# Feed-forward norm without its mean, scale and shift on the activations: one transposed set for two products

## The chip, the cores and the metric

One core of one Trainium2 chip runs the whole program. The metric is the device time of one execution in microseconds (us). Engines: TensorE (PE, matmuls and transposes), VectorE (DVE), ScalarE (ACT), GpSimd (POOL), and the queue that issues the DMAs (SP). All data are fp32.

## The reference

Eight images of 32x32 positions with 128 channels go through two layers. Layer 0: layer norm, full self-attention over the 1024 positions with 8 heads of 16, output product, residual. Layer 1, on the same 1024 tokens:

```
tokens = x @ Win + b_in
t      = layernorm(tokens) * g1 + be1          # queries, pooled keys and values
attn   = attention of all queries on the 16 best of 64 pooled keys
tokens = tokens + attn                         # "tok2" in the kernel
t2     = layernorm(tokens) * g2 + be2
ff     = gelu(t2 @ Wf1 + bf1) @ Wf2 + bf2
out    = (tokens + ff) @ Wout + bout
```

with layernorm(x) = (x - mean) * rsqrt(var + 0.001). The kernel computes out as tok2 @ Wout + gelu(...) @ (Wf2 @ Wout) + a constant row (`out_bias`), with Wf2 @ Wout (`w2o`) folded at the start.

## The kernel before, in words

An image's 1024 tokens are 8 tiles of 128, its heads 4 pairs. The main loop `image(n)` of each engine runs over n = 0 to 7 and, inside, over 32 steps s (a pair of heads times a tile of keys). At each step TensorE makes the attention scores of image n (L636, into the tile S, in two halves c), ScalarE takes their exponentials (L904, Pr), and TensorE multiplies these with V (L651, O; in most images for two steps together, in images 0, 7 and the start of 1 for one). Into every step other work is woven, in an order written out by hand and the same on all engines:

- `before_tasks(n, s)`: layer 0's norm, transposes and products of image n + 1 (input transposes L584 at steps 6 and 10, evicted by ScalarE to xhT and xnT; the product `tokx`, by `by_token` L665 with A<-win_s, drained by VectorE at L1049 at steps 32 and 37, that is steps 0 and 5 of the next loop). The transposes of step 6 reuse PSUM bank A and wait for that drain.
- `after_tasks(n, s)`: layer 1 of image n. Its steps 0 to 31 run in the loop of image n + 1, its steps 32 to 43 in the loop of image n + 2. The step numbers are in the tuples USUAL (images 0 to 5) and ENDING (images 6 and 7). After the last loop, `tail()` lists the steps that are left: image 6's 32 and 33, image 7's 0 to 3, image 6's 34 to the end, then image 7's. Image 7 (LAST) works by itself there, its TensorE kept busy by matmuls without use (L888, WARM).

Each engine executes its own instructions in this order; semaphores tie the engines together. Layer 1's products go through two PSUM banks, BC[0] and BC[1], in turns numbered by `b_turns`: `b_turn` makes TensorE wait until the turn before on that bank is drained, `drain_b` makes an evicting engine wait until it is filled.

The end of layer 1, for image n < 7, in USUAL's step numbers:

- `tok` (3): the product of the attention output with `wow` (L665, BC<-wow,attnT) gives the tokens. It waits for the DMAs (SP, L366) that bring the attention output of the image whose loop has just ended, in transposed form, after `divide_o` (L1130 to L1137) on VectorE. VectorE adds (L1158), takes statistics (L1019) and makes mean and 1/deviation in some eighteen operations on 128x8 values (`layer_norm`, L1026 to L1043), into ln1; `norm1` (8) normalises (L1146, eight operations).
- `tok2` (31): VectorE adds the layer-1 attention to the tokens, in a tile that shares E2's memory (the profile prints E); statistics. `layer_norm` again at 32, into the same ln1.
- `tt2` (33): eight transposes of the raw tokens tok2 (L657, BC<-ident,E), copied by ScalarE into tok2T, a name for Y's memory (L932, Y<-BC). ScalarE first waits for the store of the image before (out_done).
- `norm2` (34): VectorE writes `that` = (tok2 - mean) / deviation (L1146). `t2` (37): eight transposes of it (L657, BC<-ident,that), and ScalarE's evictions into tT multiply by g2 and add be2 (L919).
- `ff` (39): TensorE's products with Wf1 (L765), VectorE's evictions with bf1 into hT (L1302), ScalarE's gelu (L953) with a table load before and behind.
- `wout` (40): tok2T times Wout into both BC banks (L772). `out` (41 and 43): hT times w2o is accumulated on top (L780), one bank each, and VectorE evicts with `out_bias` into Y (L1311). SP stores Y in the next loop.

In ENDING the same steps are tt2 29, norm2 30, t2 32, ff 33, wout 34, out 35 and 36; image 7 accumulates its output in A and O.

## Time and profile before

| | us |
|---|---|
| median of 3 runs (lowest, highest) | 808.82 (807.91, 809.05) |
| the profiled execution | 811.36 |
| its span, first to last instruction | 809.6 |
| mean granted TensorE clock in it | 0.985 |
| busy: TensorE, ScalarE, VectorE, GpSimd | 762.6, 605.2, 503.5, 162.2 |
| exponentials L904, 512 of them, mean | 1029 ns |
| loop of image 3, by the starts of its exponentials | 282.5 to 374.6 |

The rows in the section further down are copied from the profile. A row of the timeline gives the start and the length of a merged group of instructions in us, then the engine, the line, the operation, what it writes and reads with the shapes, how many there are, and in brackets the idle time of the engine before it and what ended it. "issue" stands for idle time that no other engine's work ended. TensorE's fp32 products show as two instructions each. Times run from the first instruction.

### The profile page before, as it was taken

To read this page: it belongs to the slowest core of one execution; us is meant where nothing else is said; L and a number is where in the kernel's file an instruction comes from. 1 tells how busy PE (TensorE), PEld (TensorE's weight loads), DVE (VectorE), ACT (ScalarE), POOL (GpSimd) and SP (SyncE) were. 2 spreads that over 40 slices of the span, in tenths; PEclk is the share of its full clock that TensorE was granted. 3 is DMA by queue.
4 is the path that set the end of the run, shared out by engine and by line. 5 is a ranking of instruction groups with operands and counts; after the bars stand their busy time and mean duration, and the time that the engine had idled before them with its cause. 6 is when DMAs were issued, how large, how long until landed. Compare 5 with 4: busy or idle time off the path is not lost.

```text
span 809.6 us, 14186 instructions
## 1 busy us (share of the span) xinstructions
PE 762.6 (94%) x5001; PEld 364.6 (45%) x5001; DVE 503.5 (62%) x1512; ACT 605.2 (75%) x686; POOL 162.2 (20%) x198
## 2 busy tenths in 40 slices
PE   7889988999999999999999999999999998999967
PEld 5522333345443545345543555345453544334655
DVE  5512545678657775678657775677736783466764
ACT  3597779787887788787987788878887867876313
POOL 2530503410331221410321212410310201100000
PEclk8999999999999999999999999999999999999979
DMA  2543243532433342522523333422414332400100
GB/s 64 105 81 82 51 67 72 105 51 43 94 69 75 55 69 51 121 51 44 101 54 82 64 57 63 111 49 48 77 36 103 66 53 41 109 9 2 32 1 27
DMA packets 44732, 51.32 MB, mean 63 GB/s; under 512 B 15728, under 2 KB 33776, under 8 KB 44656
## 3 DMA queue, kind: packets, MB, share of 16 engines
q1 hardware_dynamic: 44656, 50.35, 32.2%
q8 instruction: 42, 0.69, 0.4%
q14 instruction: 34, 0.28, 0.1%
HBM read 5.45 MB, written 4.19 MB: 12 GB/s over the span
## 4 chain that ended last, share of the span: by engine, by line
PE 61%; ACT 15%; issue 6%; DVE 5%; ACTq 0%; DVEq 0%
PE O L651 21%; PE S L636 15%; ACT Pr L904 10%; PE BC L665 6%; PE BC L657 3%; PE BC L706 2%; PE BC L765 2%; PE BC L684 2%; PE A L665 2%; PE BC L780 2%; PE A L589 2%; ACT hT L953 1%; ACT L904 1%; ACT L953 1%; ACT E L938 1%
## 5 line engine op out<-in xcount | busy, mean ns | idle before, releaser
L904 ACT ACTIVATE Pr<-S 128x1024 f32<-128x1024 f32 x512 | 491.5, 1029 | 116.0 <-PE S L636 112.3
L651 PE MATMUL O<-Pr,Va 128*32 128x512 f32 x2048 | 255.0, 602 | 1.6 <-DVE OT L1130 0.9
L636 PE MATMUL S<-Qs,Ks 49*128 49x512 f32 x1024 | 216.0, 468 | 23.9 <-ACT Pr L904 21.8
L636 PEld LDWEIGHTS S<-Qs,Ks 49*128 49x128 f32 x1024 | 87.1, 184 | 170.8 <-ACT Pr L904 135.5
L651 PEld LDWEIGHTS O<-Pr,Va 128*32 128x32 f32 x2048 | 49.6, 109 | 103.5 <-issue 95.8
L1130 DVE STREAM_TRANSPOSE OT<-O 128x512 f32<-128x512 f32 x32 | 22.8, 714 | 55.4 <-PE O L651 55.2
L1235 DVE TENSOR_REDUCE r<-BC 128x1 f32<-128x512 f32 x56 | 35.9, 683 | 17.3 <-PE BC L706 17.3
L478 POOL TENSOR_SCALAR xn<-X,ln 128x128 f32<-128x128 f32 x56 | 45.8, 829 | 3.3 <-DVE ln L1043 3.3
L517 POOL TENSOR_TENSOR q1l<-q1T,q1h 128x1024 fp32r<-128x1024 f32 x7 | 16.7, 2381 | 142.1 <-DVE q1h L1187 142.1
L509 POOL TENSOR_TENSOR squares<-qh 128x1024 bf16<-128x1024 f32 x7 | 13.3, 1893 | 153.0 <-DVE hot L1257 112.8
L531 POOL TENSOR_TENSOR tokx<-tokx_new,tok_bias 128x1024 f32<-128x1024 f32 x8 | 18.9, 2366 | 120.0 <-DVE tokx_new L1049 120.0
L919 ACT ACTIVATE tT<-BC,cols 128x512 f32<-128x512 f32 x32 | 23.4, 778 | 22.6 <-PE BC L657 22.6
L500 POOL TENSOR_SCALAR tokx_new<-win_sum,ln 128x128 f32<-128x128 f32 x64 | 37.4, 605 | 1.4 <-POOL tokx L531 1.3
L1302 DVE TENSOR_SCALAR hT<-BC,cols 128x512 f32<-128x512 f32 x28 | 21.0, 751 | 23.2 <-PE BC L765 21.7
L489 POOL COPY Va<-v_new 128x256 f32<-128x256 f32 x32 | 11.8, 399 | 115.0 <-PE O L651 95.2
L1311 DVE TENSOR_TENSOR Y<-BC,out_bias 128x512 f32<-128x512 f32 x14 | 9.6, 690 | 36.5 <-PE BC L780 36.5
L589 PE MATMUL A<-xnT,wqkv_s 128*128 128x512 f32 x56 | 31.5, 645 | 0.0
L765 PE MATMUL BC<-tT,wf_s 128*128 128x512 f32 x56 | 27.5, 614 | 1.1 <-ACT tT L919 0.5
L780 PE MATMUL BC<-w2o,hT 128*128 128x128 f32 x224 | 28.4, 280 | 0.0
L780 PEld LDWEIGHTS BC<-w2o,hT 128*128 128x128 f32 x224 | 26.0, 192 | 4.7 <-issue 4.7
L706 PE MATMUL BC<-Q1s,K1s 96*128 96x512 f32 x56 | 24.1, 510 | 0.0
L1137 DVE STREAM_TRANSPOSE On<-OT 128x512 f32<-128x512 f32 x32 | 22.8, 711 | 1.1
(232 smaller groups left out, 986.9 us busy)
## 6 DMA issues: line engine op xcount, KB each, us to landing
Qs<-qh SPq DMA_DIRECT2D x128, 64.0 KB, 2.3
Ks<-kh SPq DMA_DIRECT2D x128, 64.0 KB, 2.3
Q1s<-q1h SPq DMA_DIRECT2D x56, 128.0 KB, 2.4
X<-in_x_dram SPq DMA_DIRECT2D x8, 512.0 KB, 4.1
Qs<-ql SPq DMA_DIRECT2D x64, 64.0 KB, 2.3
Ks<-kl SPq DMA_DIRECT2D x64, 64.0 KB, 2.3
attnT<-On SPq DMA_DIRECT2D x128, 32.0 KB, 2.0
out_dram<-Y SPq DMA_DIRECT2D x16, 256.0 KB, 2.8
```

The costliest lines, as they stand in the source:

```text
L478: ins = pool.tensor_scalar(xn[:, t, :], X[:, t, :], ln[:, 0, t:t + 1], ln[:, 1, t:t + 1], ALU.subtract, ALU.mult)
L500: ins = pool.tensor_scalar(tokx_new[:, t, :], win_sum[:, :], ln0[n % 2][:, 0, t:t + 1], None, ALU.mult)
L589: pe.matmul(A[:, :], wqkv_s[:, c:c + C], half(xnT, h), start=True, stop=True).then_inc(a_filled, 1)
L636: mm = pe.matmul(S[:, c, a * HALF:(a + 1) * HALF], Ks[head, j, kb * P:(kb + 1) * P], Qs[head, j, c * HALF:(c + 1) * HALF], start=True, sto ...
L651: mm = pe.matmul(O[r:r + 32, :], Va[:, kb, 2 * j + a, :], Pr[:, (STEPS * n + s) % 3, c, a * HALF:(a + 1) * HALF], start=(kb == 0), stop=(k ...
L657: mm = pe.transpose(bank[:, t * P:(t + 1) * P], src[:, 4 * h + t, :], ident[:, :])
L665: mm = pe.matmul(bank[:, t * P:(t + 1) * P], lhs[:, c:c + P], w, start=(i == 0), stop=(i == len(pairs) - 1))
L706: pe.matmul(bank[:, :], K1s[0:ROWS1, j, :, :].rearrange("p a b -> p (a b)"), half(Q1s[0:ROWS1, j, :], h), start=True, stop=True).then_inc( ...
L765: pe.matmul(bank[:, :], wf1_s[:, f * C:(f + 1) * C], half(tT, h), start=True, stop=True)\
L780: mm = pe.matmul(bank[:, t * P:(t + 1) * P], hT[:, f, c:c + P], w2o[:, f, :], start=False, stop=(t == 3 and f == 1))
L904: act.activation(Pr[:, g % 3, c, :], S[:, c, :], ACT.Exp, scale=SCALE).then_inc(probs_ready, 1)
L1235: ins = dve.tensor_reduce(r8[:, 2 * j + h:2 * j + h + 1], bank[:, :], AX.X, ALU.max)
```

## The change

- `scaled_form` takes the place of `normal_form` at norm2: `that` = tok2 / deviation, the mean stays in.
- Since sum over channels of (x - mean) * g2 * Wf1 is a product of x with a weight whose column means are taken off, Wf1 becomes g2 * Wf1 less its column means, and be2 @ Wf1 is added to bf1. That is done once, in the loop of image 1: VectorE scales before the loop, TensorE multiplies by all ones and by be2 at step AT_FOLD = 1, VectorE subtracts and adds.
- The eviction at t2 becomes a plain copy. tT now holds the transposed tokens over their deviation.
- For n < 7 the raw tokens' transposes and copies (tt2) go. `wout` multiplies tT with Wout, in a turn of its own (K_WOUT); VectorE drains it in eight operations that multiply by the deviation (a further result of `layer_norm`, ln2's row 6) and add out_bias, into Y. VectorE, no longer ScalarE, waits for out_done.
- `out` starts its own accumulation, each half in its own turn (K_OUT), and VectorE adds it to Y.
- The second norm's values are in a tile ln2 of their own. Image 7 keeps its raw transposes and its accumulated output, with the changed norm and weight.

```diff
--- before.py
+++ after.py
@@ -96,7 +96,8 @@
 WAKE = 24
 
 K_TOK, K_T, K_Q1, K_PK, K_PV, K_SC, K_RT, K_RB, K_SELK, K_SELV = 0, 2, 4, 6, 7, 8, 16, 17, 18, 19
-K_S2, K_PT, K_TOK2, K_TT2, K_T2, K_FF, K_OUT = 20, 22, 24, 26, 28, 30, 34
+K_S2, K_PT, K_TOK2, K_TT2, K_T2, K_FF, K_OUT, K_WOUT = 20, 22, 24, 26, 28, 30, 34, 36
+AT_FOLD = 1
 FIRST_STEPS = 18
 
 
@@ -122,8 +123,9 @@
                 (at.tt2, K_TT2, 2), (at.t2, K_T2, 2))
     return ((at.tok, K_TOK, 2), (at.t, K_T, 2), (at.q1, K_Q1, 2), (at.pk, K_PK, 2),
             *((at.sc[j], K_SC + 2 * j, 2) for j in range(PAIRS)), (at.rt, K_RT, 1), (at.rb, K_RB, 1), (at.sel, K_SELK, 2),
-            (at.s2, K_S2, 2), (at.pt, K_PT, 2), (at.tok2, K_TOK2, 2), (at.tt2, K_TT2, 2), (at.t2, K_T2, 2),
-            *((at.ff[f], K_FF + 2 * f, 2) for f in range(2)), (at.wout, K_OUT, 2))
+            (at.s2, K_S2, 2), (at.pt, K_PT, 2), (at.tok2, K_TOK2, 2), (at.t2, K_T2, 2),
+            *((at.ff[f], K_FF + 2 * f, 2) for f in range(2)), (at.wout, K_WOUT, 2),
+            (at.out[0], K_OUT, 1), (at.out[1], K_OUT + 1, 1))
 
 
 def b_turns():
@@ -197,7 +199,7 @@
 
         tok, tT, q1T = sb("tok", [P, TILES, C]), sb("tT", [P, T]), sb("q1T", [P, T])
         hT, that = sb("hT", [P, 2, T]), sb("that", [P, TILES, C])
-        st1, ln1 = sb("st1", [P, TILES, 6]), sb("ln1", [P, 8, TILES])
+        st1, ln1, ln2 = sb("st1", [P, TILES, 6]), sb("ln1", [P, 8, TILES]), sb("ln2", [P, 8, TILES])
         pooled, pkv = sb("pooled", [P, POS]), sb("pkv", [POS, 2 * C])
         q1h, q1l = sb("q1h", [P, T], f32r), sb("q1l", [P, T], f32r)
         Q1s = sb("Q1s", [ROWS1 + 1, PAIRS, T], f32r)
@@ -214,6 +216,7 @@
 
 
         E2T = hT[:, 1, :]
+        wf1_scaled = hT[:, 0, 0:FF]
         k1_last = [K1s[:, i, :, :].rearrange("p a k -> p (a k)") for i in range(2)]
         Qt = q1h[:, 0:HALF].rearrange("p (j q) -> p j q", j=PAIRS)
         tok2T, tok2 = Y[:, :, :].rearrange("p t c -> p (t c)"), E2[:, :, :].rearrange("p (t g) k -> p t (g k)", t=TILES)
@@ -258,6 +261,7 @@
         q1h_ready, q1l_ready, q1_stacked = sem("q1h_ready"), sem("q1l_ready"), sem("q1_stacked")
         pooled_ready, hot_ready = sem("pooled_ready"), sem("hot_ready")
         out_done = sem("out_done")
+        ff_scaled, ff_summed, ff_folded = sem("ff_scaled"), sem("ff_summed"), sem("ff_folded")
         last_filled, last_ff, last_out = sem("last_filled"), sem("last_ff"), sem("last_out")
 
         sp_passed, pool_passed, pe_passed, dve_passed = sem("sp_passed"), sem("pool_passed"), sem("pe_passed"), sem("dve_passed")
@@ -668,7 +672,15 @@
 
             def after_tasks(n, s):
                 at = plan(n)
+                if n == 0 and s == AT_FOLD:
+                    pe.wait_ge(ff_scaled, 1)
+                    pe.matmul(BC[0][:, 0:FF], all_ones[:, :], wf1_scaled, start=True, stop=True)
+                    for f in range(2):
+                        mm = pe.matmul(BC[1][:, f:f + 1], wf1_s[:, f * C:(f + 1) * C], BE2, start=True, stop=True)
+                    mm.then_inc(ff_summed, 1)
                 if s == at.tok:
+                    if n == 0:
+                        pe.wait_ge(ff_folded, 1)
                     for side in range(2):
                         pe.wait_ge(attn_in[side], 16 * ATTN_DMAS * (PAIRS // 2) * (n + 1))
                     for h in range(2):
@@ -735,7 +747,7 @@
                     for h in range(2):
                         b_ready(n, K_PT + h)
                         by_token(*b_turn(n, K_TOK2 + h), [(E2T, bd_v[:, :, :].rearrange("p a b -> p (a b)"))], h)
-                if s == at.tt2:
+                if s == at.tt2 and n == LAST:
                     for h in range(2):
                         b_ready(n, K_TOK2 + h)
                         turn4(*b_turn(n, K_TT2 + h), tok2, h)
@@ -766,19 +778,16 @@
                             .then_inc(filled, 1)
                 if s == at.wout and n < LAST:
                     for h in range(2):
-                        bank, filled = b_turn(n, K_OUT + h)
-                        for t in range(4):
-                            c = (4 * h + t) * P
-                            pe.matmul(bank[:, t * P:(t + 1) * P], tok2T[:, c:c + P], wout_s[:, :], start=(t == 0), stop=False)
+                        by_token(*b_turn(n, K_WOUT + h), [(tT, wout_s[:, :])], h)
                 if s in at.out:
                     h = at.out.index(s)
-                    bank, filled = (OUT_BANKS[h], last_filled) if n == LAST else (BC[h], b_filled[h])
+                    bank, filled = (OUT_BANKS[h], last_filled) if n == LAST else b_turn(n, K_OUT + h)
                     for f in range(2):
                         pe.wait_ge(gelu_ready, 2 * n + 1 + f + (2 * h if n == LAST else 0))
                         for t in range(4):
                             c = (4 * h + t) * P
                             mm = pe.matmul(bank[:, t * P:(t + 1) * P], hT[:, f, c:c + P], w2o[:, f, :],
-                                           start=False, stop=(t == 3 and f == 1))
+                                           start=(n < LAST and t == 0 and f == 0), stop=(t == 3 and f == 1))
                     mm.then_inc(filled, 1)
 
             def last_scores():
@@ -913,17 +922,20 @@
             def after_tasks(n, s):
                 at = plan(n)
                 if s in (at.t, at.t2):
-                    g, be, k0 = (G1, BE1, K_T) if s == at.t else (G2, BE2, K_T2)
+                    k0 = K_T if s == at.t else K_T2
                     for h in range(2):
                         bank, drained = drain_b(n, k0 + h)
-                        act.activation(half(tT, h), bank[:, :], ACT.Identity, bias=be, scale=g).then_inc(drained, 1)
+                        if s == at.t2:
+                            act.activation(half(tT, h), bank[:, :], ACT.Copy).then_inc(drained, 1)
+                        else:
+                            act.activation(half(tT, h), bank[:, :], ACT.Identity, bias=BE1, scale=G1).then_inc(drained, 1)
                 if s == at.q1:
                     if n > 0:
                         act.wait_ge(q1_stacked, 16 * STACK1_DMAS * n)
                     for h in range(2):
                         bank, drained = drain_b(n, K_Q1 + h)
                         act.activation(half(q1T, h), bank[:, :], ACT.Copy).then_inc(drained, 1)
-                if s in (at.pt, at.tt2):
+                if s == at.pt or (s == at.tt2 and n == LAST):
                     dst, k0 = {at.pt: (E2T, K_PT), at.tt2: (tok2T, K_TT2)}[s]
                     if s == at.tt2 and n > 0:
                         act.wait_ge(out_done, 2 * 16 * n)
@@ -1136,6 +1148,16 @@
                     dve.wait_ge(attn_in[j % 2], 16 * ATTN_DMAS * (PAIRS // 2 * n + j // 2))
                 dve.transpose(On[:, j % 2, :], OT[:, :, :].rearrange("p q e -> p (q e)")).then_inc(on_ready, 1)
 
+            def scaled_form(own, src, n, k):
+
+                for h in range(2):
+                    dve.wait_ge(b_filled[h], b_after(n, k + h))
+                dve.wait_ge(own[0], own[1] + own[2])
+                for t in range(TILES):
+                    ins = dve.tensor_scalar(that[:, t, :], src[:, t, :], ln2[:, 1, t:t + 1], None, ALU.mult)
+                    if t % 4 == 3:
+                        ins.then_inc(that_ready, 1)
+
             def normal_form(own, src, n, k):
 
                 if n >= 0:
@@ -1151,6 +1173,10 @@
             def after_tasks(n, s):
                 at = plan(n)
                 own = own_after
+                if n == 0 and s == AT_FOLD:
+                    dve.wait_ge(ff_summed, 1)
+                    dve.scalar_tensor_tensor(out=wf1_s[:, :], in0=BC[0][:, 0:FF], scalar=-1.0 / C, in1=wf1_scaled, op0=ALU.mult, op1=ALU.add)
+                    dve.tensor_tensor(cols[:, 8:10], cols[:, 8:10], BC[1][:, 0:2], ALU.add).then_inc(ff_folded, 1)
                 if s == at.tok:
                     dve.wait_ge(tokx_moved, n + 1)
                     for h in range(2):
@@ -1290,10 +1316,10 @@
                         dve.wait_ge(drained, b_after(n, K_TOK2 + h))
                     step(own, statistics(tok2, st1))
                 if s == at.norm2 - 2:
-                    layer_norm(own, st1, ln1, LN1_EPS, after_done)
+                    layer_norm(own, st1, ln2, LN1_EPS, after_done, deviation=True)
                     own[2] += 1
                 if s == at.norm2:
-                    normal_form(own, tok2, n, K_T)
+                    scaled_form(own, tok2, n, K_T)
                 for f in range(2 if n < LAST else 0):
                     if s != at.ff[f]:
                         continue
@@ -1301,13 +1327,26 @@
                         bank, drained = drain_b(n, K_FF + 2 * f + h)
                         dve.tensor_scalar(hT[:, f, h * HALF:(h + 1) * HALF], bank[:, :], cols[:, 8 + f:9 + f], None, ALU.add)\
                             .then_inc(drained, 1)
-                if s in at.out:
+                if s == at.wout and n < LAST:
+
+                    if n > 0:
+                        dve.wait_ge(out_done, 2 * 16 * n)
+                    for h in range(2):
+                        bank, drained = drain_b(n, K_WOUT + h)
+                        for i in range(4):
+                            t = 4 * h + i
+                            ins = dve.scalar_tensor_tensor(out=Y[:, t, :], in0=bank[:, i * C:(i + 1) * C], scalar=ln2[:, 6, t:t + 1],
+                                                           in1=out_bias[:, :], op0=ALU.mult, op1=ALU.add)
+                        ins.then_inc(drained, 1)
+                if s in at.out and n < LAST:
                     h = at.out.index(s)
-                    if n == LAST:
-                        dve.wait_ge(last_filled, 4 + h)
-                        bank, drained = OUT_BANKS[h], last_out
-                    else:
-                        bank, drained = drain_b(n, K_OUT + h)
+                    bank, drained = drain_b(n, K_OUT + h)
+                    dve.wait_ge(drained, b_after(n, K_WOUT + h))
+                    dve.tensor_tensor(flat4(Y, h), bank[:, :], flat4(Y, h), ALU.add).then_inc(drained, 1)
+                if s in at.out and n == LAST:
+                    h = at.out.index(s)
+                    dve.wait_ge(last_filled, 4 + h)
+                    bank, drained = OUT_BANKS[h], last_out
                     dve.tensor_tensor(tiles4(Y, h), bank[:, :].rearrange("p (t c) -> p t c", t=4),
                                       out_bias[:, :].unsqueeze(1).to_broadcast([P, 4, C]), ALU.add).then_inc(drained, 1)
 
@@ -1390,6 +1429,8 @@
             image(0)
 
             dve.wait_ge(weights_in, 16 * WEIGHT_DMAS)
+            dve.tensor_scalar(wf1_scaled, wf1_s[:, :], G2, None, ALU.mult).then_inc(ff_scaled, 1)
+            dve.wait_ge(ff_scaled, 1)
             for n in range(1, IMAGES):
                 image(n)
             for n, s in tail():
```

## Rows read from the trace of the kernel before

**Rows 1.** The page: busy us and share; the chain by engine.

```profile
PE 762.6 (94%) x5001; PEld 364.6 (45%) x5001; DVE 503.5 (62%) x1512; ACT 605.2 (75%) x686; POOL 162.2 (20%) x198
...
PE 61%; ACT 15%; issue 6%; DVE 5%; ACTq 0%; DVEq 0%
```

**Rows 2.** Timeline, TensorE, scores at the end of image 5's loop.

```profile
558.31 0.73 PE L636 MATMUL S<-Qs,Ks 49*128 49x512 f32 x4
```

**Rows 3.** Timeline, start of image 6's loop.

```profile
558.85 3.77 ACT L904 ACTIVATE Pr<-S 128x1024 f32<-128x1024 f32 x4 [2.45 <-PE S L636]
...
561.27 1.09 PE L657 MATMUL BC<-ident,E 128*128 128x128 f32 x8
...
562.29 0.89 PE L636 MATMUL S<-Qs,Ks 49*128 49x512 f32 x4
562.48 1.12 ACT L932 ACTIVATE Y<-BC 128x512 f32<-128x512 f32 x2
...
564.97 1.03 PE L636 MATMUL S<-Qs,Ks 49*128 49x512 f32 x4
...
565.93 2.05 PE L665 MATMUL BC<-wow,attnT 128*128 128x128 f32 x16
```

**Rows 4.** Timeline, TensorE, image 5's token product.

```profile
474.19 2.02 PE L665 MATMUL BC<-wow,attnT 128*128 128x128 f32 x16 [0.57 <-issue]
```

**Rows 5.** Timeline, image 6: VectorE ahead of the input transposes.

```profile
574.08 0.17 DVE L1037 TENSOR_TENSOR ln<-ln 128x8 f32<-128x8 f32 x1
...
574.28 0.17 DVE L1038 SCALAR_TENSOR_TENSOR ln<-ln 128x8 f32<-128x8 f32 x1
574.37 1.12 DVE L1049 SCALAR_TENSOR_TENSOR tokx_new<-A,ln,tokx_new 128x128 f32<-128x128 f32 x4
...
575.64 0.63 PE L584 MATMUL A<-ident,xn 128*128 128x128 f32 x4
```

**Rows 6.** Groups by shape: xcount | busy us, mean ns.

```profile
L695 PE MATMUL BC<-wkv_s,pooled 128*64 128x256 f32 x16 | 5.2, 404 | 0.0
```

**Rows 7.** Timeline, TensorE, image 1's scores of step 2.

```profile
110.14 0.91 PE L636 MATMUL S<-Qs,Ks 49*128 49x512 f32 x4
```

**Rows 8.** Groups by shape, normalisation, one-pointer operation, both evictions.

```profile
L919 ACT ACTIVATE tT<-BC,cols 128x512 f32<-128x512 f32 x32 | 23.4, 778 | 22.6 <-PE BC L657 22.6
...
L1146 DVE TENSOR_SCALAR that<-E,ln 128x128 f32<-128x128 f32 x64 | 17.1, 340 | 1.1
...
L932 ACT ACTIVATE Y<-BC 128x512 f32<-128x512 f32 x16 | 9.0, 622 | 2.7 <-PE BC L657 2.7
...
L1257 DVE TENSOR_SCALAR hot<-iota_f,rank 64x128 f32<-64x128 f32 x8 | 2.2, 279 | 0.3
```

**Rows 9.** Timeline, image 3, steps 8 and 9.

```profile
308.95 0.71 DVE L1137 STREAM_TRANSPOSE On<-OT 128x512 f32<-128x512 f32 x1
...
310.66 2.05 PE L780 MATMUL BC<-w2o,hT 128*128 128x128 f32 x16
```

**Rows 10.** Timeline, image 7, steps 1 to 3.

```profile
654.85 1.09 ACT L932 ACTIVATE Y<-BC 128x512 f32<-128x512 f32 x2 [0.39 <-PE BC L657]
...
659.25 2.05 PE L665 MATMUL BC<-wow,attnT 128*128 128x128 f32 x16
```

**Rows 11.** Timeline, end of image 7's loop.

```profile
739.97 3.78 ACT L904 ACTIVATE Pr<-S 128x1024 f32<-128x1024 f32 x4
...
746.41 3.99 PE L765 MATMUL BC<-tT,wf_s 128*128 128x512 f32 x8 [0.52 <-ACT tT L919]
```

**Rows 12.** Timeline, the tail.

```profile
755.37 3.74 PE L780 MATMUL BC<-w2o,hT 128*128 128x128 f32 x32
...
758.92 1.28 DVE L1311 TENSOR_TENSOR Y<-BC,out_bias 128x512 f32<-128x512 f32 x2
```

**Rows 13.** Busy us by stretch, tail: PE, PEld, DVE, ACT, POOL, clock, DMA.

```profile
769.83:773.24 3.41, 0.43 (x8) 0.00 (x0) 3.41 (x4) 0.00 (x0) 0.00 (x0) 1.00 0.01 2
773.24:783.48 10.24, 8.13 (x33) 6.36 (x35) 5.77 (x18) 0.57 (x1) 0.00 (x0) 0.50 0.01 2
```

## The prediction, made before the changed kernel was run

> **What bounds the kernel now.** I read the busy totals and the chain first: TensorE is busy 94% of the span and its lines hold 61% of the chain, ScalarE's 15% [rows 1]. That suggests that every matmul removed is time gained. But an average can't tell what a given step waits for, and the change touches four places only. So I read the timeline engine by engine there: the start of an image's loop (steps 0 to 6, where the raw transposes stand), steps 8 and 9 (the two products into the output), the loop of image 7, and the tail.
>
> At the start of an image the order is: two steps' exponentials (four operations) run back to back from 558.85 for 3.77 us, the 8 raw transposes take TensorE from 561.27 to the next scores at 562.29, and those scores stretch to 0.89 us, where scores that wait for nothing take 0.73 [rows 2], because they wait for the last of the four. The two copies on ScalarE cost 1.12 us, and the scores of step 3 wait for the exponentials behind them (1.03 us instead of 0.73). Then comes the token product, at 565.93 [rows 3]. In image 5 this product has 0.57 us of idle time before it that no engine ended [rows 4], and images 3 and 4 show the same, shorter: it waits for the last DMA of the previous image's attention output, which has nothing to do with the change. From there VectorE is the late one: layer norm, tokx drain, and TensorE's transposes of the next input start at 575.64, right after VectorE's drain ends at 575.49 (574.37 + 1.12) [rows 5].
>
> **The change part by part.** All in us against the profiled execution.
>
> A. Fold, once, in image 1. New on TensorE: one 128x128 by 256 product and two with a single moving column. Nearest row: a 256-wide product is two instructions and takes 0.65 (5.2 over 8 images) [rows 6]; the narrow ones lie between nothing and the same each, so 0.65 to 1.95. There ScalarE is the fuller engine: the scores of step 2 take 0.91 where 0.73 is undisturbed [rows 7], and the scores of steps 1 and 3 show similar slack, some 0.5 to 0.8 in all, while the token product follows without a wait. I take 1.1 for the work and +0.5 for the time (0 to +1.9). VectorE's scaling and its two small additions stand in front of nothing: its token step comes 5 us later.
>
> B. Images 2 to 6, steps 0 to 6. Eight transposes go (1.02 of TensorE each image) and two copies (1.12 of ScalarE). TensorE without them reaches the scores of step 2 early, but the second half of these still waits for the fourth exponential, which ends at 562.62 (558.85 + 3.77) whatever TensorE does. So the product with V behind them starts when it did. What does come earlier are the exponentials of step 2, so the scores of step 3 need 0.73 and not 1.03: 0.3 is all that is gained ahead of the token product, and where the DMA lands late (images 3, 4, 5) it is gained for nothing. Behind that stands VectorE: the norm gets one dependent operation more (+0.20, the distance between two such operations [rows 5]), its eight normalisations have one pointer scalar instead of two; 340 ns each now, and the nearest row with one pointer and one operation is 279 [rows 8], so -0.06 each, -0.5 together. That is -0.3 net (bounds +0.2, if they stay at 340, and -0.5). So image 2 and image 6 give 0.3 each, the three between nothing: -0.6. Ends: -5.1, if 5 x 1.02 came off whole, and +1.0, if VectorE only grows.
>
> C. Images 2 to 6, steps 8 and 9. Output banks used to be filled by both products in one accumulation. Now the first product has to be drained by eight small VectorE operations before the second may start. VectorE is then in the division of the attention output until 309.66 (308.95 + 0.71), and the drain queues behind it. A comparable operation (PSUM in, one pointer scalar, one tensor) has four in 1.12 [rows 5], so half 0 is free at some 310.7, and with about 0.1 for the semaphore the second product starts at 310.84 instead of 310.66 [rows 9]: +0.18 an image, +0.9 for five (0 to +2). The remaining four and the queued normalisations of the next image finish near 314; their reader, eight transposes at step 12, comes 7 us later. The final addition is the same size as before. VectorE also takes over ScalarE's wait for the store of the image before; that store is issued right behind the step-13 transfers of the loop before, most of a loop earlier, so this wait is 0; if it weren't, the drains, the normalisations and half of TensorE's step 9 would queue behind it.
>
> D. Image 7, steps 1 to 7. Here the weighted values run each step, and no input transposes follow, so VectorE isn't the gate. ScalarE sits idle 0.39 for the raw transposes and spends 1.09 on the copies; step 2's exponentials queue behind, TensorE's scores of step 3 wait for those, and the token product is at 659.25 [rows 10]. Without transposes and copies this goes 1.2 forward. Then ScalarE's eviction at step 5 turns from scale-and-bias (0.78 each) into a plain copy (0.62 by the copy row) [rows 8]; the two gate the exponentials that gate the scores and the feed-forward, -0.3 more. D is -1.5 (0 to -2.2).
>
> E. End of image 7's loop. The same transposes and copies of image 6 (ENDING's step 29) stand before the last four exponentials, which start at 739.97 behind the copies; they can start at 739.0: -0.95. The transposes of the scaled tokens follow, and the feed-forward at 746.41 waits 0.52 for ScalarE's eviction [rows 11], which becomes shorter: -0.25. E is -1.2 (-0.9 to -2.1).
>
> F. The tail. The written order puts image 7's token norm (steps 0 to 3) before image 6's step 34. Today TensorE does both products of image 6 while VectorE is in that norm, the second from 755.37 to 759.11 (3.74), and when VectorE comes out of the norm at 758.92 it only has two additions (1.28) before it normalises image 7 at some 760.15 [rows 12]. After the change VectorE has to come out of the norm first, then drain: half 0 at 758.92 + 1.13 = 760.05; TensorE's 16 matmuls from 760.17 to 762.05 and the next 16 to 763.9 (half of the 3.74 each); the last addition half of 1.28 more, normalisation at 764.55. That is +4.4 on a chain on which image 7 has nothing else to run. Ends: +2.3, if only the eight drains counted, and +5.
>
> G. Last norm. +0.20, -0.24 up to the first half's fourth tile, and a plain copy (-0.18) before the last feed-forward: -0.2.
>
> H. TensorE's clock. In F TensorE idles from some 755.5 to 760.2, 4.7 long. The trace has one such pause: after a stretch of 3.41 with 0.43 busy in it the granted clock was 0.50 for 10.24 (1.2 GHz of 2.4) [rows 13]. At that level the 32 matmuls would take twice 3.74, so a fall costs up to +1.9 for each 3.74 that it lasts; part of it can fall into the pause itself. None costs 0. I take +0.8.
> The Trainium skill, page TensorE: Matmul & The Clock Gate, section Part 1: The HAM clock gate (the "warmup" mystery), says that the slow clock is the default state and that only activity lifts it. By that rule the pause is answered nearly always and in full, and the sum is 1.1 higher.
>
> Sum: 0.5 - 0.6 + 0.9 - 1.5 - 1.2 + 4.4 - 0.2 + 0.8 = +3.1. The profiled execution took 811.36 (span 809.64 and 1.7 around it) and would take 814.5; the median of the runs shown is 808.82, 0.3% lower, and the same sum gives 811.9.
>
> **The rivals.** (1) TensorE's pace decides, as its 94% says: then B is -5.1 and the wait in C is taken up by a stream that has got shorter (0); with A, D to H as above the sum is 0.5 - 5.1 - 2.7 + 4.4 - 0.2 + 0.8 = -2.3, 806.5; faster. Its place is step 1 of images 2 to 6, and it decides wherever the scores of step 3 wait neither for an exponential nor for the DMA, and the input transposes of step 6 not for VectorE. Against it stand exactly these waits [rows 3 to 5]; for it, that TensorE's gaps there add up to under 1 us an image. (2) The tail costs only its drains (F = +2.3, H = 0), because TensorE's and VectorE's halves overlap better than in my walk, and B gives 0.3 in each image: 0.5 - 1.5 + 0.9 - 2.7 + 2.3 - 0.2 = -0.7, 808.1, no difference. Against it: the second product can't start before the drain, nor the addition before the product. (3) VectorE becomes the gate in every image: the normalisations stay at 340 ns (B +1.0), the drains reach the second product 0.4 late (C +2.0), and the clock falls in full (H +1.9): 0.5 + 1.0 + 2.0 - 2.7 + 4.4 - 0.2 + 1.9 = +6.9, 815.7. For it: VectorE goes from one operation into the next over the whole start of an image.
>
> **How the numbers follow.** Forecast as summed 0.55; rival 1 0.15; rival 2 0.18; rival 3 0.12. Range 806.0 to 815.5: it takes in rival 1's own value and leaves out its far end and rival 3's upper half. The forecast alone spans 809.8 to 813.8. A difference under 0.2% (1.6 us) is what the measurement can't tell from none. Faster 0.14 (nearly all of rival 1), same 0.22 (rival 2 and the low edge of the forecast), slower 0.64.
>
> **What would show it.** In the after-trace: token product of images 2 and 6 earlier by 0.3 relative to the loop's start, of 3 and 5 not; input transposes at step 6 right behind VectorE's tokx drain or not moved; the second product of step 9 started by a VectorE drain; image 7's loop shorter by about 2.5; a pause of more than 4 us on TensorE between the two products of image 6, and the clock's answer to it. If the images 2 to 6 are shorter by 0.8 or more each, B is wrong and with it the forecast; if image 7's normalisation isn't some 3 us later relative to its token product, F is.

## The result, and the profile after

The changed kernel took 815.53 us (median of 5, 814.11 to 817.07), the kernel before 809.05 in the same comparison (median of 5, 807.91 to 810.85): ratio 1.0074, 95% interval 1.0051 to 1.0097. It is slower by 6.5 us where +3.1 was forecast, and 815.53 lies on the upper edge of the range (815.5). The profiled execution of it took 816.37 (span 814.4), that of before 811.36 (span 809.64).

The page of the changed kernel, busy time and chain; compare [rows 1]:

```profile
PE 758.3 (93%) x4951; PEld 360.1 (44%) x4951; DVE 515.5 (63%) x1579; ACT 595.7 (73%) x672; POOL 162.4 (20%) x198
...
PE 61%; ACT 15%; issue 6%; DVE 5%; ACTq 0%; DVEq 0%
```

TensorE has 4.3 us less to do, ScalarE 9.5 less, VectorE 12 more. None of it says why the time rose; the chain's shares are unchanged to the percent. The stretches do. I cut both spans at the first exponential of each image:

```
                start  im.0   im.1   im.2   im.3   im.4   im.5   im.6   im.7   tail
before          31.56  75.17  83.87  91.91  92.07  91.91  92.37  91.83  93.06  65.89
changed         29.25  75.17  85.26  93.20  91.67  91.99  93.62  91.77  89.73  72.75
```

The largest item is the tail. Timeline of the changed kernel, TensorE and VectorE (columns: start, length, instruction, idle time before it); it answers to [rows 12]:

```profile
751.22 2.05 PE L669 MATMUL BC<-wout_s,tT 128*128 128x128 f32 x16
...
752.09 1.64 DVE L1031 BATCH_NORM_STATS2 st<-tok 128x6 f32<-128x128 f32 x8
...
756.57 0.17 DVE L1050 SCALAR_TENSOR_TENSOR ln<-ln 128x8 f32<-128x8 f32 x1
756.66 2.16 DVE L1338 SCALAR_TENSOR_TENSOR Y<-BC,ln,out_bias 128x128 f32<-128x128 f32 x8
...
757.84 6.73 PE L789 MATMUL BC<-w2o,hT 128*128 128x128 f32 x32 [4.57 <-DVE Y L1338]
761.66 0.69 DVE L1345 TENSOR_TENSOR Y<-BC,Y 128x512 f32<-128x512 f32 x1 [2.84 <-PE BC L789]
...
764.61 0.69 DVE L1345 TENSOR_TENSOR Y<-BC,Y 128x512 f32<-128x512 f32 x1 [2.26 <-PE BC L789]
765.21 1.88 DVE L1168 TENSOR_SCALAR that<-tok,ln 128x128 f32<-128x128 f32 x7
```

The first product ends at 753.27; its drains (L1338) wait behind image 7's norm until 756.66, TensorE stands idle for 4.57, and image 7's normalisation starts 8.55 after its norm where it started some 1.2 after it before. The 32 matmuls of the second product take 6.73 where they took 3.74. Why, the same stretch shows by windows (busy PE, PEld, DVE, ACT, POOL, then the granted clock, DMA share, GB/s):

```profile
750.00:757.11 7.11, 3.27 (x28) 2.93 (x26) 5.96 (x30) 0.27 (x1) 0.00 (x0) 1.00 0.00 0
757.11:763.94 6.83, 6.10 (x28) 6.11 (x29) 2.40 (x8) 0.00 (x0) 0.00 (x0) 0.50 0.08 27
763.94:768.00 4.06, 3.85 (x30) 2.70 (x28) 2.74 (x9) 0.77 (x1) 0.00 (x0) 1.00 0.27 85
```

The clock fell to 0.50 (1.2 GHz of 2.4) just before the product began and stayed there for nearly all of it.

The second item I had not looked for. The start of image 5's loop in the changed kernel, TensorE alone, then the windows around it:

```profile
468.53 0.50 PE L640 MATMUL S<-Qs,Ks 49*128 49x512 f32 x2 [0.28 <-ACT Pr L913]
...
469.45 0.51 PE L640 MATMUL S<-Qs,Ks 49*128 49x512 f32 x2 [0.41 <-ACT Pr L913]
...
470.36 0.80 PE L640 MATMUL S<-Qs,Ks 49*128 49x512 f32 x2 [0.41 <-ACT Pr L913]
...
471.09 3.24 PE L655 MATMUL O<-Pr,Va 128*32 128x512 f32 x16
```

```profile
466.54:470.39 3.85, 2.74 (x18) 1.55 (x16) 3.11 (x9) 3.85 (x5) 0.14 (x1) 1.00 0.04 7
470.39:473.80 3.41, 3.41 (x18) 0.85 (x18) 2.91 (x21) 1.83 (x2) 0.00 (x0) 0.50 0.18 37
473.80:478.00 4.20, 4.20 (x36) 2.61 (x32) 3.24 (x11) 2.50 (x3) 0.00 (x0) 1.00 0.53 85
```

Where the raw transposes stood [rows 3], TensorE now has short waits for exponentials between pairs of score matmuls. At 470.39 the clock falls for 3.41 us, just as the longest run of products with V (L655) of that stretch begins: 3.24 for the 16 that take 1.92 in the undisturbed loops. Image 2's loop has the same at 193.91. Steps 0 to 6 of these two loops take 19.9 us where the other three take 18.3 to 18.4, some 1.6 more; the kernel before has no such fall in images 2 to 6.

### The profile page after: what moved, and what is told of

Read it like the earlier page. It is cut to its first block, busy times and chain, and to the rows that moved or that the text cites. A ratio compares the mean times of both kernels' runs of the same rounds, so it can differ in the third digit from the quotient of the medians.

```text
span 814.4 us, 14153 instructions
## 1 busy us (share of the span) xinstructions
PE 758.3 (93%) x4951; PEld 360.1 (44%) x4951; DVE 515.5 (63%) x1579; ACT 595.7 (73%) x672; POOL 162.4 (20%) x198
## 4 chain that ended last, share of the span: by engine, by line
PE 61%; ACT 15%; issue 6%; DVE 5%; ACTq 0%; DVEq 0%
PE O L655 22%; PE S L640 15%; ACT Pr L913 11%; PE BC L669 6%; PE BC L789 3%; PE BC L661 3%; PE BC L718 2%; PE BC L777 2%; PE BC L696 2%; PE A L669 2%; PE A L593 2%; ACT hT L965 1%; ACT L913 1%; ACT L965 1%; ACT E L950 1%
## 5 line engine op out<-in xcount | busy, mean ns | idle before, releaser
L655 PE MATMUL O<-Pr,Va 128*32 128x512 f32 x2048 | 257.1, 606 | 1.9 <-ACT Pr L913 1.0
L655 PEld LDWEIGHTS O<-Pr,Va 128*32 128x32 f32 x2048 | 50.0, 109 | 105.1 <-issue 94.9
L1261 DVE TENSOR_REDUCE r<-BC 128x1 f32<-128x512 f32 x56 | 36.0, 684 | 19.2 <-PE BC L718 19.2
L521 POOL TENSOR_TENSOR q1l<-q1T,q1h 128x1024 fp32r<-128x1024 f32 x7 | 16.7, 2390 | 143.4 <-DVE q1h L1213 143.4
L789 PE MATMUL BC<-w2o,hT 128*128 128x128 f32 x224 | 31.4, 299 | 4.6 <-DVE Y L1338 4.6
L789 PEld LDWEIGHTS BC<-w2o,hT 128*128 128x128 f32 x224 | 28.9, 209 | 9.8 <-DVE Y L1338 6.3
L1345 DVE TENSOR_TENSOR Y<-BC,Y 128x512 f32<-128x512 f32 x14 | 9.7, 690 | 29.9 <-PE BC L789 29.9
L931 ACT ACTIVATE tT<-BC,cols 128x512 f32<-128x512 f32 x16 | 11.7, 775 | 22.9 <-PE BC L661 22.8
L718 PE MATMUL BC<-Q1s,K1s 96*128 96x512 f32 x56 | 23.9, 507 | 1.8 <-issue 1.8
```

The source lines that it names most:

```text
L655: mm = pe.matmul(O[r:r + 32, :], Va[:, kb, 2 * j + a, :], Pr[:, (STEPS * n + s) % 3, c, a * HALF:(a + 1) * HALF], start=(kb == 0), stop=(k ...
L718: pe.matmul(bank[:, :], K1s[0:ROWS1, j, :, :].rearrange("p a b -> p (a b)"), half(Q1s[0:ROWS1, j, :], h), start=True, stop=True).then_inc( ...
L789: mm = pe.matmul(bank[:, t * P:(t + 1) * P], hT[:, f, c:c + P], w2o[:, f, :], start=(n < LAST and t == 0 and f == 0), stop=(t == 3 and f = ...
L1261: ins = dve.tensor_reduce(r8[:, 2 * j + h:2 * j + h + 1], bank[:, :], AX.X, ALU.max)
```

## The experiments

Twelve kernels ran, all timed against the kernel before on the same chip. Beside each time stands the half-clock time, twice the span times (1 - mean granted clock): the microseconds of an execution that TensorE spent at the lower level. It is worth having because it differs between executions of one kernel: over 89 executions of the kernel before (in three groups) it runs from 9.7 to 30.9 us, and the time follows it as 803.3 + 0.34 x half-clock time, with a correlation of 0.92. (A correlation: a late transfer, too, can both lengthen an execution and let the clock fall, so not all of the slope need be the clock's doing.) A profile shows one draw from this; the means show the kernel.

**The changed kernel again** (label c1), beside three variants.

> The changed kernel once more, as the yardstick for the others of this set. In its first profile TensorE's clock fell to 0.5 for 3.41 us at the start of two of the five middle loops (images 2 and 5), where scores wait for exponentials since the transposes went; each such loop is 1.65 us longer. Theory clock (the pause that the transposes used to fill lets the clock fall): falls again in some of the loops of images 2 to 6, at step 1 or 2, not always the same ones; total +6 to +7 us over the kernel before. Rival chance (the falls belong to that one execution): none in the middle loops, total about +3.

It took 816.89 (5 runs; ratio 1.0099, 1.0081 to 1.0116), 8.2 more than the kernel before. Its profile has the falls at the start of the loops again, now of images 2 and 3, so they don't belong to the first execution alone. Mean half-clock time 29.7 us against 17.9 of the kernel before (19 runs; 808.65); in the first comparison it was 25.1. At 0.34 a microsecond the clock would account for 4.0 of the difference here and, against the same 17.9, for 2.4 in the first; some 4 would be left for the rest of the change.

**Unread transposes as filler.** TensorE transposes the raw tokens as before; nobody reads them, and ScalarE copies nothing.

```diff
+                if s == at.tt2 and n < LAST:
+                    for h in range(2):
+                        b_ready(n, K_TOK2 + h)
+                        for t in range(4):
+                            pe.transpose(BC[h][:, t * P:(t + 1) * P], tok2[:, 4 * h + t, :], ident[:, :])
```

> The eight raw transposes stay on TensorE in images 0 to 6, written into the two banks that are free at that step, and nobody evicts or reads them; all else as in the changed kernel. Theory clock: no falls in the middle loops, each of them as short as the undisturbed ones of the changed kernel (steps 1 to 6 in 16.4 to 16.6 us) although TensorE does 1.02 us more, so 1.7 us a fall is saved, -2 to -4 us against the changed kernel with 1 to 2.5 falls an execution. Rival pace (TensorE's work decides): +5 to +7 us. Rival chance: no difference or up to +1 (image 7).

815.01 (6 runs, 811.78 to 819.87; ratio 1.0074, 1.0045 to 1.0104): no gain that this measurement can tell. But its trace answers the question on the middle loops. Start of image 5's loop, TensorE:

```profile
470.03 0.50 PE L640 MATMUL S<-Qs,Ks 49*128 49x512 f32 x2 [0.28 <-ACT Pr L918]
470.46 1.09 PE L754 MATMUL BC<-ident,E 128*128 128x128 f32 x8
471.49 0.87 PE L640 MATMUL S<-Qs,Ks 49*128 49x512 f32 x4
472.28 1.92 PE L655 MATMUL O<-Pr,Va 128*32 128x512 f32 x16
```

The transposes stand exactly where TensorE waits otherwise, so they cost the loop nothing (steps 0 to 6, median of images 2 to 6 against the undisturbed loops: 18.26 us with them, 18.27 without), and no clock fell in images 2 to 6. In image 7, where products with V run in every step, they are not free: steps 0 to 6 take 18.76 with them, 17.72 without. The clock fell for 3.41 in image 0, where the changed kernel had no fall, and for 6.83 in the tail, where it did.

**The tail's order.** Image 6's first product is issued before image 7's steps 0 to 3, so that its drains come ahead of image 7's norm in VectorE's queue.

```diff
-    k, m = ENDING.wout - STEPS, ENDING.tok + 1
+    k, m = ENDING.wout - STEPS + 1, ENDING.tok + 1
```

> In the tail the product with Wout of image 6 and its drain (step 34) stand before image 7's token steps 0 to 3 instead of behind them; nothing else changes. Theory tail (the product waits for a drain that is queued behind image 7's norm, and the pause costs the clock): the pause of 4.57 us ahead of the second product goes, the token step is 1 us later, the normalisation of image 7 some 6 us earlier: -5 to -6.5 us, so about the time of the kernel before. Rival (the tail's length is in what follows the normalisation and the clock falls anyway): less than -2.

812.32 (12 runs; ratio 1.0035, 1.0020 to 1.0050): 3.2 less than the changed kernel's 815.53 and 4.6 less than its 816.89, short of the 5 to 6.5 expected. The tail is 68.37 instead of 72.75. Timeline:

```profile
751.06 3.84 PE L789 MATMUL BC<-w2o,hT 128*128 128x128 f32 x32
...
756.50 1.28 DVE L1345 TENSOR_TENSOR Y<-BC,Y 128x512 f32<-128x512 f32 x2
757.70 2.13 DVE L1168 TENSOR_SCALAR that<-tok,ln 128x128 f32<-128x128 f32 x8
...
758.86 2.14 PE L661 MATMUL BC<-ident,that 128*128 128x128 f32 x8 [1.92 <-DVE that L1168]
```

The second product takes 3.84 and no longer waits; two additions stand between norm and normalisation, as before. A new pause of 1.92 ahead of the next transposes brought a fall of its own (8 transposes in 2.14 instead of 1.09).

**The pause filled and not removed.** 32 useless matmuls between the two products, the order as changed.

```diff
+                    for _ in range(16 if n == LAST - 1 else 0):
+                        for a in range(2):
+                            head = slice(64 * a, 64 * a + MROW + 1)
+                            pe.matmul(S[:, 0, a * HALF:(a + 1) * HALF], Ks[head, 0, 0:P], Qs[head, 0, 0:HALF], ...)
```

> The order of the tail stays, but 32 matmuls without use (16 pairs, some 3.6 us) run on TensorE between the two products of image 6. Theory clock: the pause no longer lowers the clock, the 32 matmuls of the second product take 3.8 instead of 6.73 us: -3 us against the changed kernel. The waiting for the drain stays. Rival (only the queue costs, the clock comes back in time): 0 to +0.5.

812.82 (9 runs, 810.53 to 820.25; ratio 1.0037, 1.0021 to 1.0053). No fall at the two products; the tail is 69.70, 3.05 less than in the changed kernel. As the queue is untouched, that is the clock's part: 3.0 against this execution of the changed kernel. Against its other one (c1) it is 1.9: there the pause was 4.57 too, but the fall lasted 3.41, the second product took 5.46 and the tail 71.60. Its profiled execution had three falls in images 2 to 6 and one of 13.65 us in image 7's loop. No other profile has one of that length; it begins at 706.38, at the end of a pause of 1.35 on TensorE ahead of the product with the stacked queries (see A below on that wait), and what makes it so long stays open.

**All mended, with and without filler.** Both have the tail's new order and do the fold in image 0's loop (scaling at step 24, sums at 26, correction at 28, `AT_FOLD = 26`); the first also has the unread transposes for images 0 to 5.

> The changed kernel with three things put right at once: the first output product of image 6 is issued before image 7's steps 0 to 3 in the tail, the fold (scaling, sums, correction) is done in image 0's loop at steps 24 to 28 instead of image 1's step 1, and in the tasks of images 0 to 5 the eight raw transposes stay on TensorE, read by nobody. Theory (queue in the tail plus TensorE's clock, which falls in the middle loops because step 1 of each lost eight transposes): 815.5 to 816.9 less 4.4 (tail order, measured alone as 3.2 to 4.6), less 1.0 (fold: step 1 of image 1's loop back from 3.10 to about 2.1), less 1 to 2 (no fall in images 2 to 6): 809.5, half-clock time per execution about 18 us as in the kernel before. Rival (falls are chance, the transposes' absence has nothing to do with them): no gain from the filler, 811.3, the same as its sister kernel without filler, half-clock time the same in both. Second rival (what is left is VectorE's own added work): over 812 in both.

> The same kernel without the unread transposes: tail order and early fold alone. Theory: falls of TensorE's clock at steps 1 to 2 of some loops of images 2 to 6 remain, one to three per execution, so 1 to 2 us more than the kernel with filler: 811.3 (812.3 of the tail order alone, less 1.0 for the fold), half-clock time about 24 us. Rival (falls are chance): equal to the kernel with filler within 0.5 us and in half-clock time.

811.02 (12 runs; 1.0017, 0.9999 to 1.0035) and 810.90 (12 runs; 1.0035, 1.0010 to 1.0061): the same medians, and 1.5 more than the 809.5 expected with filler. The means differ, 810.44 and 811.96, as do the half-clock times, 21.8 and 25.3; with 12 scattered runs that is a hint. The fold in image 1 costs +1.0 in its step 1 (3.10 instead of 2.13); moved, that step is back at 2.13, but image 0's steps 26 to 29 grow by some 0.5. Half of the cost moved with it.

**The kernel before, thinned.** Everything as before, but of the raw transposes of images 0 to 5 one of four, then none (the diff shows the first):

```diff
                         b_ready(n, K_TOK2 + h)
-                        turn4(*b_turn(n, K_TT2 + h), tok2, h)
+                        bank, filled = b_turn(n, K_TT2 + h)
+                        pe.transpose(bank[:, 0:P], tok2[:, 4 * h, :], ident[:, :]).then_inc(filled, 1)
```

> The kernel before, with only one of each four raw transposes left in the tasks of images 0 to 5 (it leaves out the transposes of three quarters of the tokens; ScalarE's copies, all waits and all the rest stay). TensorE loses some 6 of 8 transposes in step 1 of the loops of images 2 to 7 and nothing else changes. Theory: TensorE's clock now falls in steps 1 to 2 of these loops here too, one to three times per execution, half-clock time up from about 15 to 18 to 21 to 28 us, and the time does not go down but up by 0.5 to 2.5: 810. Rival (falls have another cause, such as the folded norm's shorter VectorE work or the later product): no more falls than the kernel before has, and the time at or below 808.65.

> The kernel before without any of the eight raw transposes in the tasks of images 0 to 5 (it leaves out the transposes of the raw tokens; the two signals, ScalarE's copies and all the rest stay). With six of eight left out only one of five loops showed a fall and the half-clock time did not rise (median 15.4 us against 17.8). Theory, as it stands after that run (the clock falls only where all eight are gone): falls in a third of the loops, half-clock time 21 us or more, 810 to 811. Rival (something else in the changed kernel, such as the second product's second wait or the shorter normalisation, takes part): half-clock time again about 15 to 18, time 809 or less.

With one of four left: 809.53 (12 runs; 1.0013, 0.9999 to 1.0028), one fall in five loops, half-clock time not longer (mean 16.2 against 16.7). With none: 810.64 (12 runs; 1.0004, 0.9980 to 1.0028), two falls in five loops, half-clock time again not longer (18.1 against 19.2). Windows of image 4's loop in the latter:

```profile
373.78:378.01 4.23, 3.12 (x18) 1.71 (x16) 3.19 (x9) 4.20 (x6) 0.15 (x1) 1.00 0.04 10
378.01:381.42 3.41, 3.41 (x18) 0.59 (x16) 2.86 (x20) 2.38 (x4) 0.00 (x0) 0.50 0.16 34
```

So the fall at this place needs nothing of the change but the transposes' absence: it comes in the kernel before too. How often it comes per execution the half-clock times don't confirm; my expectation of 21 us and more failed twice. And neither thinned kernel is faster than before: with less work TensorE gains nothing here, which is what [rows 3 to 5] said. The times alone would not settle that, since falls and late transfers (see A below) could hide a gain; steps 0 to 6 do: in loops without a fall they take 18.62 to 18.69 in the thinned kernels, and 18.61 to 18.70 in three of the five before, 18.87 and 19.16 in the other two, where the token product's transfer was late.

**Pause ahead of image 7's transposes.** 12 instead of 8 pairs of warming matmuls (`ENDING.t: 12`), with filler and without:

> The first kernel of this batch with 12 instead of 8 pairs of useless matmuls ahead of image 7's transposes of the normalised tokens in the tail, to fill the new pause of 1.92 us that the tail order alone showed there (with a fall of 3.41 us, which made the eight transposes 2.14 us and the token product's successors slow). Theory: pause filled, no fall there, 0.5 to 1.5 less than the kernel without: 808.7. Rival: the pause comes from VectorE's queue and the clock has little to do on that stretch: the same time within 0.3.

> The same mended kernel with 12 warming pairs without the unread transposes in the middle loops (and without the 8 further pairs). With the earlier pair (811.02 with, 810.90 without, means of half-clock time 21.8 and 25.3 us) it weighs the unread transposes a second time. Theory (without them the clock falls in some middle loops): 1 to 2 us over 808.83, half-clock time 3 to 6 us longer. Rival (the falls of the middle loops are chance): within 0.5 us of 808.83 with the same half-clock time.

808.83 (12 runs; 1.0001, 0.9983 to 1.0020) with, 811.61 (12 runs; 1.0027, 1.0004 to 1.0050) without. With filler the kernel is where the kernel before is. Mean half-clock times 17.1 (before: 16.7 in that group) and 24.3 (before: 19.2 in its own). The fall at the pause is gone from both profiles, and the tails are 67.53 and 67.30 where the pair without the further matmuls had 68.66 and 68.59; the mean time over that of the kernel before went from 1.5 to 0.0 us with filler and from 3.1 to 2.3 without. Taken together, the two pairs weigh the filler: 24 executions with it average 0.8 us over the kernel before of their own group, 24 without it 2.7; the difference is 1.9 us, with a 95% interval of about 0.5 to 3.3, and the half-clock time differs by 4.1 us. The start of image 5's loop without filler and of image 4's with it, windows:

```profile
464.30:468.53 4.23, 3.11 (x18) 1.71 (x16) 3.50 (x12) 4.22 (x5) 0.14 (x1) 1.00 0.04 9
468.53:471.94 3.41, 3.41 (x18) 0.59 (x16) 2.83 (x20) 1.38 (x2) 0.00 (x0) 0.50 0.26 48
```

```profile
375.74:379.50 3.76, 3.48 (x24) 2.38 (x22) 3.02 (x8) 3.76 (x4) 0.13 (x1) 1.00 0.03 6
379.50:383.00 3.50, 3.50 (x28) 1.40 (x27) 3.01 (x21) 2.57 (x4) 0.00 (x0) 1.00 0.16 36
```

Over all profiles, falls at the start of a loop (3.8 to 5.1 us in) of images 2 to 6: with the transposes, read or unread, 0 in 30 loops (six profiles, four of them of changed kernels with filler); changed kernels without them 10 in 30 (six profiles); the thinned kernels before 1 and 2 in 5. Each makes steps 0 to 6 of its loop 1.2 to 1.7 us longer than in its kernel's undisturbed loops.

**The next pause.** TensorE stands idle for 4.38 us later in the tail while VectorE reduces the scores, and the 10.24 us at half clock of [rows 13] follow. Eight pairs of useless matmuls go there, in the mended kernel and in the kernel before:

```diff
+                if s == at.rt and n == LAST:
+                    b_ready(n, K_SC)
+                    for _ in range(8):
+                        ...
```

> The kernel with all of it mended and 12 warming pairs (808.83), and 8 further pairs of useless matmuls in the tail ahead of the one-row transpose of image 7's pooled maxima, where TensorE stood idle for 4.38 us and after which the clock was at half for 10.24 us (the s2 product x16 3.75 us instead of about 1.9, eight warming pairs 2.07 instead of about 1.03, two selection products and one short product about 0.5 dearer). Theory (clock is what that stretch lost): the fall goes or is shortened, 1.5 to 3 us less: 806.5, half-clock time some 7 to 10 us less. Rival: 8 pairs cover only the end of the pause, the clock falls as before and the time is the same, 808.8.

> The kernel before with only the 8 further pairs of useless matmuls ahead of the same one-row transpose in the tail. It tells whether what they bring belongs to the change or to either kernel. Theory: the same gain as in the changed kernel, 1.5 to 3 us: 806.6. Rival: no gain, 808.9.

In the mended kernel, windows:

```profile
769.00:773.69 4.69, 3.10 (x24) 1.85 (x21) 3.06 (x13) 0.00 (x0) 0.00 (x0) 1.00 0.00 0
773.69:777.10 3.41, 3.29 (x15) 3.02 (x15) 1.33 (x4) 0.00 (x0) 0.00 (x0) 0.50 0.00 0
777.10:785.00 7.90, 6.60 (x54) 5.32 (x52) 5.92 (x10) 2.46 (x4) 0.00 (x0) 1.00 0.00 0
```

The fall shrank from 10.24 to 3.41 in both, as expected, and the tails by 0.8 (67.53 to 66.70) and 0.6 (65.89 to 65.25). The times: 808.28 (12 runs; 0.9987, 0.9965 to 1.0009) against 810.07, and 809.89 (12 runs; 0.9999, 0.9979 to 1.0020). I expected 1.5 to 3 us, and 7 to 10 us less at half clock in the mended kernel; what came is too small to be told from nothing, and the mean half-clock time fell by 3.4 (13.7). One reason stands in the trace: the 3.41 us that are left of the fall lie on the product that VectorE waits for. The kernel before, TensorE, and the mended one with the further matmuls:

```profile
779.38 3.75 PE L665 MATMUL BC<-bd_k,q1T 128*128 128x128 f32 x16
```

```profile
774.24 3.39 PE L669 MATMUL BC<-bd_k,q1T 128*128 128x128 f32 x16
```

At the full clock sixteen 128x128 matmuls take 2.05 [rows 3]. Most of the rest of that chain is VectorE's and keeps its length (the longest reduction takes 2.29 in both). No version that ran is shown to beat the kernel before.

## Why the prediction was right in direction and short in size

By its own steps, measured in the profiled executions; "undisturbed" means loops without a fall of the clock.

A, +0.5: step 1 of image 1's loop grew by 0.97. ScalarE had less slack than I read: the products themselves took what the estimate said.

```profile
107.84 0.70 PE L677 MATMUL BC<-hT,all_ones 128*128 128x256 f32 x2
...
108.38 0.50 PE L679 MATMUL BC<-cols,wf_s 128*128 128x1 f32 x4
108.81 0.73 PE L640 MATMUL S<-Qs,Ks 49*128 49x512 f32 x4
```

Another 0.4 in image 1 is at step 18, where the first product with the stacked queries (L718) waits for their transfer. No term of the prediction had this. Image 4 of the changed kernel, TensorE, then the queue that issues the transfers, there and in image 3, where nothing waits:

```profile
429.25 0.70 PE L718 MATMUL BC<-Q1s,K1s 96*128 96x512 f32 x2 [0.41 <-issue]
```

```profile
418.58 6.24 SPq L358 DMA_DIRECT2D Q1s<-q1h  x8
```

```profile
327.05 5.77 SPq L358 DMA_DIRECT2D Q1s<-q1h  x8
```

The eight issues take longer; in the kernel before they take 4.94 to 5.21 in images 2 to 6, and over all profiles the wait appears in these images where they take more than some 5.8 (one exception, with 5.77). It goes with the transposes' absence too: a loop of images 2 to 6 is late there in 5 of 30 with the transposes, read or unread, and in 24 of 40 without, the thinned kernels among them; in image 7 the wait comes one step earlier, in none of six profiles with and all eight without. In this profile it costs 0.4 in image 1, 1.2 in images 2 to 6 and 0.4 in image 7. Why the issues take longer stays open.

B, -0.6: right on VectorE, wrong on the transfer. Steps 0 to 6 take 18.27 instead of 18.70 (medians over images 2 to 6, loops with a fall left out), the token product of the undisturbed loops stands 6.77 after the loop's start (7.08 in image 6 before), the normalisation has the price forecast, 282 ns [rows 8 had 279], and the input transposes follow VectorE's tokx drain in image 4 as in [rows 5]:

```profile
L1157 DVE TENSOR_SCALAR that<-E,ln 128x128 f32<-128x128 f32 x64 | 13.3, 282 | 1.1
```

```profile
389.50 1.12 DVE L1061 SCALAR_TENSOR_TENSOR tokx_new<-A,ln,tokx_new 128x128 f32<-128x128 f32 x4
...
390.97 0.66 PE L588 MATMUL A<-ident,xn 128*128 128x128 f32 x4
```

But I gave the gain to images 2 and 6 alone, because in images 3 to 5 the token product waited for its transfer. That wait belonged to the one execution: before, the product stood at 7.41, 7.25 and 7.70 in images 3 to 5; in another profile of the same loops (the kernel before with the useless matmuls in the tail) at 7.07, 7.69 and 7.06; after, at 6.77 in images 3 and 4. Those two gained 0.47 and 0.44 in steps 0 to 6 where nothing was forecast, and the five together some 2.5 with the falls taken out.

C, +0.9: smaller. The second product starts right behind the scores, with only its weight load waiting for the drain; step 9 grew by 0.07 an image, not 0.18:

```profile
309.49 2.12 DVE L1338 SCALAR_TENSOR_TENSOR Y<-BC,ln,out_bias 128x128 f32<-128x128 f32 x8
...
310.63 1.86 PEld L789 LDWEIGHTS BC<-w2o,hT 128*128 128x128 f32 x16 [0.31 <-DVE Y L1338]
310.63 2.05 PE L789 MATMUL BC<-w2o,hT 128*128 128x128 f32 x16
```

B and C together were forecast at +0.3; the three undisturbed loops average 91.81 against 92.02, so -1.0 for five: 2.5 gained in steps 0 to 6, 0.3 lost at step 9, 1.2 at the late transfers.

D, -1.5: step 1 of image 7's loop lost 1.20 and step 5 0.37, -1.57. E, -1.2: step 29 lost 1.01, step 30 gave back 0.33; -0.7. The late transfer at step 17 took 0.4 of both. Image 7's loop was 3.3 shorter than before only because the profiled execution of before had a fall in it at 728.87, worth 1.5; against a loop without one (91.60, in the kernel before with the useless matmuls in the tail) it is 1.9.

F, +4.4: right. Of the 7.35 by which image 7's normalisation moved away from its norm, 3.0 is the slower second product and 4.35 the queue. The reordering and the filled pause confirm the split: the tail went down by 4.38 when both went (a new fall included), and by 3.05 when only the clock's part went.

G, -0.2: the tail grew by 6.86 where the queue and the clock make 7.35, so all the rest of it is 0.5 shorter; I have not split that.

H, +0.8: the step that failed, twice over. In the tail the clock's answer cost 3.0: it was not one product's worth at half price, because the fall began 0.73 before the product did and lasted for nearly the whole of it, 6.73 for 3.74; my bound of +1.9 for each 3.74 of fall was right as a rate, and I took a small part of one where nearly two came. The execution of the profile was also a dear one: behind the same pause of 4.57 the product took 5.46 in c1 (a fall of 3.41) and 5.87 with the filler (6.83, of which 2.55 fell into the pause), 1.7 and 2.1 more than at the full clock. The clock answered that pause in all three; none cost as little as 0.8. And I looked for the clock only at the one long pause. The places where the change takes TensorE's work away while ScalarE sets the pace, step 1 of the middle loops, had no term at all; they cost 1.6 for each fall, two of them in this profile.

Without the clock the steps sum to +2.3 as forecast (0.5 - 0.6 + 0.9 - 1.5 - 1.2 + 4.4 - 0.2), and as measured to about +2.4 (1.4 in image 1, -1.0, -1.9, and 3.9 in the tail). That the two agree is in part luck: some 2.0 of late transfers, which had no term, stand against 1.9 more gained in B and 0.6 less lost in C than forecast. The clock makes the rest. In the profiles its falls cost the changed kernel 6.2 (3.0 + 2 x 1.6), and the kernel before 3.8 that the changed one's execution didn't have (6.83 us of fall at 12.07 and 3.41 at 25.72 where the changed one has a single 3.41, with a start 2.3 longer, and the fall at 728.87, 1.5): 2.4 + 6.2 - 3.8 = 4.8, the distance of the two spans. Between typical executions the changed kernel has 7 to 12 us more at half clock; at the 0.44 to 0.47 per us that the new falls cost where they lie in this profile, that is an estimated 3 to 5.5, and with the 2.4 it is 5.6 to 7.9, where 6.5 and 8.2 were measured. The regression's 0.34 is a mean over falls at all places; that less hangs on TensorE at many of them is likely and not shown.

Rival 1 (TensorE's pace decides) fell: both thinned kernels are no faster, and their steps 0 to 6 no shorter. Rival 2 (the tail costs only its drains) fell by F. Rival 3 gave 815.7, within 0.2 of what came, and not by its mechanism: VectorE's normalisations didn't stay at 340 ns, nor did the drains hold up the second product by 0.4; only its third part, the clock in full, happened, and more than in full.

## What to carry to other kernels

When a change moves a drain onto an engine that works through a queue in written order, look at where that queue's order puts it in the prologue and the tail as well as in the steady loop: here the loops gained and one step of tail order cost 4.4 us; moving it by one step gave most of it back. Before counting removed TensorE work as harmless, look at what stands around it: if the engine then waits for another between short groups of matmuls, price a fall of the clock over the work that follows. And compare means of many executions where the granted clock differs from run to run: the profile of before had one or two falls more than its typical execution.

## What the runs showed of the hardware

Unread work on TensorE can be free and still be worth keeping: eight transposes a loop cost 0.0 us in images 2 to 6 (1.0 in image 7) and went with 0 falls in 30 loops, against 10 in 30 without; over 24 executions each the kernels with them were 1.9 us faster. The kernel's time follows its half-clock time at 0.34 us per us over the whole program; where TensorE bounds the stretch it was nearer to a half: 3.0 of 6.83 and 1.7 of 3.41 in the tail, 1.6 of 3.41 in the loops. The half-clock time of an execution of one unchanged kernel varied from 9.7 to 24.3 us within one group of 35 (to 30.9 in another), and its times of 806.6 to 812.5 us in that group follow it with a correlation of 0.90.

What stays open: why the thinned kernels show falls in their profiles but no longer half-clock time over 12 executions; why the eight issues ahead of step 18 take longer where the raw transposes are gone; and the one long fall in image 7.
